# Spare TensorE passes in the last pair of heads and in the routing, and two steps of the pair moved, in a graph-transformer layer

## What is computed

```python
q, k, v = (split(xn @ W.T + b) for W, b in ((Wq, bq), (Wk, bk), (Wv, bv)))     # 16 heads of 64
phi = lambda z: (exp(z @ orf.T / 64 ** 0.25 - |z|^2 / (2 * 8)) + 1e-6) / 16      # 256 features
out = (phi(q) @ (phi(k).T @ v)) / (phi(q) @ sum(phi(k)))
x = x + gnn(xn) + out @ Wo.T + bo
g = softmax(top2(layernorm(x) @ gate_w.T + gate_b))
x = x + sum over e of g[e] * (layernorm(x) @ expert_w[e] + expert_b[e])
```

## Time and profile before

| | us |
|---|---|
| median of 3 runs | 1418.61 (1415.19 to 1418.94) |
| the profiled execution | 1417.75 |
| its span, first to last instruction | 1416.2 |
| mean granted TensorE clock | 0.973 of full |
| TensorE busy | 1354.4 (96%) |
| DVE, ACT, GpSimd busy | 789.3, 572.3, 364.1 |

### The profile page before, as it was taken

One profiled execution on the slowest core, in us unless ns is written; L12 is line 12 of the kernel. 1 busy time (PEld: TensorE's weight loads), 2 busy tenths in 40 slices (PEclk: granted clock), 3 DMA queues, 4 the chain that ended last, 5 costly groups with the idle time before them and its releaser, 6 DMA issues.

```text
span 1416.2 us, 25340 instructions
## 1 busy us (share of the span) xinstructions
PE 1354.4 (96%) x8233; PEld 1197.6 (85%) x8234; DVE 789.3 (56%) x1680; ACT 572.3 (40%) x953; POOL 364.1 (26%) x375
## 2 busy tenths in 40 slices
PE   6999999999999999999999999999999599999996
PEld 3567778999999999999999999987888588888885
DVE  7867464454466565656565656564454734444641
ACT  8543332211355454545454545451122234444440
POOL 4323333254210101010101010005023133333432
PEclk9999999999999999999999999978999599999998
DMA  5112112455200000000000000013244567777853
GB/s 185 51 49 68 42 64 68 134 158 150 64 31 16 30 15 30 15 30 15 30 15 30 15 30 0 1 60 98 72 166 148 208 183 218 220 213 211 287 134 58
DMA packets 58102, 127.78 MB, mean 90 GB/s; under 512 B 7627, under 2 KB 28827, under 8 KB 58049
## 3 DMA queue, kind: packets, MB, share of 16 engines
q1 hardware_dynamic: 48016, 96.79, 20.6%
q0 software_dynamic: 10032, 30.30, 8.7%
HBM read 91.46 MB, written 37.43 MB: 91 GB/s over the span
## 4 chain that ended last, share of the span: by engine, by line
PE 85%; DVE 5%; ACT 3%; issue 3%; DMA 1%; DVEq 0%; POOL 0%; POOLq 0%; SPq 0%; ACTq 0%
PE PB L1701 8%; PE PB L1806 7%; PE PB L1808 7%; PE PB L1807 7%; PE PB L2022 6%; PE PB L2023 6%; PE PB L2025 6%; PE PB L1844 5%; PE PB L1867 4%; PE PB L1751 3%; PE PB L1791 3%; PE PB L1752 3%; PE PB L1753 3%; PE PB L1792 3%; PE PB L1793 2%
## 5 line engine op out<-in xcount | busy, mean ns | idle before, releaser
L1806 PE MATMUL PB<-xh,hw 128*128 128x416 f32 (+1 forms) x576 | 203.8, 354 | 0.0
L1808 PE MATMUL PB<-xh,hw 128*128 128x416 f32 (+1 forms) x576 | 202.9, 352 | 0.0
L1807 PE MATMUL PB<-xl,hw 128*128 128x416 f32 (+1 forms) x576 | 202.8, 352 | 0.0
L2022 PE MATMUL PB<-mwh,mth 128*128 128x512 f32 x368 | 147.8, 402 | 0.3 <-issue 0.3
L2023 PE MATMUL PB<-mwl,mth 128*128 128x512 f32 x368 | 143.9, 391 | 0.0
L719 POOL CAST hw<-hraw 128x1024 fp32r<-128x1024 f32 x24 | 25.2, 1048 | 418.4 <-DVE qphi L1363 197.3
L1701 PE MATMUL PB<-ohs,ohd 128*128 128x512 bf16 x564 | 114.1, 349 | 0.3 <-DVE ohs L1226 0.3
L2025 PE MATMUL PB<-mwh,mtl 128*128 128x512 f32 x368 | 113.7, 390 | 0.0
L1807 PEld LDWEIGHTS PB<-xl,hw 128*128 128x128 f32 x576 | 108.6, 189 | 1.2
L1806 PEld LDWEIGHTS PB<-xh,hw 128*128 128x128 f32 x576 | 108.6, 189 | 1.2
L1808 PEld LDWEIGHTS PB<-xh,hw 128*128 128x128 f32 x576 | 108.5, 188 | 1.0
(11 more groups left out here) (304 smaller groups left out, 3103.7 us busy)
## 6 DMA issues: line engine op xcount, KB each, us to landing
mraw<-expert_w SPq DMA_DIRECT2D x64, 512.0 KB, 5.8
count_rests<-ATf POOLq DMA_DIRECT2D x9, 640.0 KB, 3.3
xrow<-x SPq DMA_DIRECT2D x40, 128.0 KB, 3.0
y_scratch<-xrow SPq DMA_DIRECT2D x40, 128.0 KB, 1.9
yrow<-y_scratch SPq DMA_DIRECT2D x20, 256.0 KB, 2.9
x2n_half<-xhat SPq DMA_DIRECT2D x20, 256.0 KB, 2.4
out<-x SPq DMA_DIRECT2D x9, 512.0 KB
ATf<-wg SPq DMA_DIRECT2D x32, 128.0 KB, 2.8
```

Source lines behind the costliest of these rows:

```text
L1806: mm(bank(i, n), hw[:, wi, 0, k, :], xh[:, k, c0:c0 + n], start=(k == 0), stop=False)
L1807: mm(bank(i, n), hw[:, wi, 0, k, :], xl[:, k, c0:c0 + n], start=False, stop=False)
L1808: ins = mm(bank(i, n), hw[:, wi, 1, k, :], xh[:, k, c0:c0 + n], start=False, stop=(k == KT - 1))
L2022: mm(y[c], mth[:, k, :], mwh[par][:, k, c * CW:(c + 1) * CW], start=(k == 0), stop=False)
```

## The change

- On TensorE, the second head's key chunk 1 stands ahead of the first head's key-value products instead of behind them, in all eight pairs.
- In the first seven pairs, the second head's query chunks 2, 3 and 4 are issued after steps 2, 4 and 6 of the projection third instead of after steps 1, 3 and 5. Chunk 5 stays behind the third.
- In the last pair, 32 spare passes of 512 columns are issued: 9 between the first head's query chunks, 7 between those of the second, 3 + 1 + 2 + 1 ahead of the four groups of transposes and 9 behind them. They write PSUM bank 0, which nothing reads any more.
- In the routing, 36 spare passes on the first expert's weights into bank 6: 4 ahead of the wait for the prefix counts' input, 20 behind these products, 12 ahead of the gates. Before the first four TensorE waits for the first slab of those weights.
- GpSimd waits for the first row tile of the output product between its split of the weights and the routing's constants.

```diff
@@ gpsimd
             split_weights(ro, 1)
+            pool.wait_ge(ro.done, 1)
             g.iota(iota8[:, :, :], [[0, TT], [1, E]], base=0, channel_multiplier=0,
@@ tensor
+            def spare(n):
+
+                for _ in range(n):
+                    mm(bank(0), orfh[:, 0:P], xh[:, 0, 0:CW], start=True, stop=True)
+
             def pair(j, last):
@@
                 turn_values(3)
+                key_features(j, 1, 1)
                 key_values(0, 0, MH * TT)
-                key_features(j, 1, 1)
                 project_third(j, 2, 0)
@@
                 if last:
                     for i in range(2, 6):
+                        spare((0, 0, 0, 2, 5, 2)[i])
                         query_features(0, i)
                     query_features(1, 0)
@@
                 if last:
                     for i in range(2, 5):
+                        spare(2)
                         query_features(1, i)
+                    spare(1)
                 else:
-                    project_third(j + 1, 0, 2, lambda k: query_features(1, 2 + k // 2) if k % 2 == 1 else None)
+                    project_third(j + 1, 0, 2, lambda k: query_features(1, 1 + k // 2) if k in (2, 4, 6) else None)
                 query_features(1, 5)
@@
+                if last:
+                    spare(3)
                 turn(0)
+                if last:
+                    spare(1)
                 turn(1)
                 if not last:
                     key_features(j + 1, 0, 0)
                     project_third(j + 1, 1, 1)
+                if last:
+                    spare(2)
                 turn(2)
+                if last:
+                    spare(1)
                 turn(3)
+                if last:
+                    spare(9)
@@
+            def meanwhile(n):
+
+                for _ in range(n):
+                    mm(bank(6), mwh0[:, 0, 0:P], mwh0[:, 0, 0:CW], start=True, stop=True)
+
+            pe.wait_ge(mw_high, 1)
+            meanwhile(4)
             pe.wait_ge(s_both, 1)
@@
             ins.then_inc(route_done, 1)
-
+            meanwhile(20)
@@
+            meanwhile(12)
             gates(0)
```

## The result

The changed kernel took 1400.05 us in the median of 5 runs (1398.57 to 1407.57), the kernel before 1418.61 us (1412.16 to 1420.43): a ratio of 0.9892, 95% interval 0.9865 to 0.9919. The forecast was 1398.4. By ratio the change is worth 14 to 15 us of the 20.2 that were summed up, by the medians of the first five runs 18.6.

The account below looks back on a forecast made before the run. TensorE, busy 96% of the span, bounds the kernel; time is won only at its waits or half clock. 3.7 + 4.2 + 12.0 + 0.3 = 20.2 us off 1417.75 gives 1397.5, as median 1398.4; range 1394.0 to 1404.5.

Parts of the forecast that it names:

- Key chunk ahead, 3.7 us: Ahead of the key-value products: the chunk fills TensorE's 0.56 us idle time, 0.46 us a pair in eight pairs.
- rival 5: Key-value products: a wait ahead of them lowers the clock in the reshaped pairs, 6.4 us a pair slower; chance 0.02.
- Query chunks one step later, 4.2 us: In the first seven pairs: issuing later covers a 0.49 us wait for ACT, 0.60 us a pair.
- The last pair, 12.0 us: Last pair through the output product's first passes: 32 spare passes keep the clock full, 12.0 us less.
- 4.9 + 0.45 + 4.05 + 0.25: Last pair's gains: to first head's outputs, to second head's outputs, their 40 products, turning the result back.
- busy 1.80 of 3.40 us: Last pair, 932.5 to 935.9: TensorE's busy time, with three waits, before the clock fell.
- narrow products with a wait of 0.49 us among them keep the clock: Ordinary pair: 6.6 us, two thirds of it 65-column products, ran at full clock despite that wait.
- GpSimd's wait, 0 us: GpSimd's wait for the first output row tile is satisfied before it is reached, costing 0.
- The routing, 0.3 us: Routing's 36 spare passes: the clock returns, falls again before the gates; only the first ten gate products gain.
- rival 1: Routing: the clock holds there too, 1.2 us more gained, 1397.2 us; chance 0.12.
- The sentence on idle gaps: Skill page ties a lost clock to longer idle gaps; by it the routing would give 1.5 us, not 0.3.

Follow-up runs that it names:

- query_step_only: Only the query chunks issued one step later, against the kernel before: 1414.51 us, median of 10, ratio 0.9996 [0.9968, 1.0023].
- the later split: Changed kernel with GpSimd's split of the next pair's key weights moved behind the turned values: 1399.02 us, ratio 0.9864 against the kernel before.
- the logits' spares: Changed kernel with the later split and eight spare passes among the last logits: 1400.33 us with 20 passes ahead of the gates, 1398.84 with 12.
- routing_only: Only the routing's 36 spare passes and GpSimd's wait, against the kernel before: 1415.23 us, median of 10, ratio 0.9985 [0.9955, 1.0015].
- chunk_ahead_only: Only the key chunk moved ahead of the key-value products, against the kernel before: 1407.96 us, median of 8, ratio 0.9943 [0.9915, 0.9972].

## Why the prediction was right, and where its terms were not

The median, 1400.05, lies 1.7 us from the forecast and inside its range; the 1404.98 of the six further runs lies 0.5 outside. Its opening says that the longest of TensorE's waits outside the routing is the 2.92 us ahead of the output product. That holds from attention on; before it the list of the kernel before has 6.2 us (line 1675, for DVE) and 4.4 us (line 1720, for ACT), which the change leaves as they are. The steps, in the order of the prediction:

1. *Key chunk ahead, 3.7 us.* The mechanism is shown: no wait, products not delayed, 0.1 us paid by the projection, 0.42 us a pair. The term was mis-sized: alone it gives about 8 us (4 to 12). What it left out is the clock. It had rival 5's price on the wrong side: a wait ahead of the narrow products that brings the clock down is a thing of the order before, seen in two ordinary pairs of `query_step_only`, at 3.2 us each where rival 5 had 6.4, and of the profiles of the new order in the first pair alone. The 10 us less at half clock are worth 3.6 us, which with the pairs' 3.4 nearly makes up the 8. That they are falls at this place is an inference, and the count speaks for a part only: two falls in five profiles are 1.3 us an execution. The execution read had no such fall, so the sum had no such term.
2. *Query chunks one step later, 4.2 us.* 0.5 to 0.6 us a pair is shown. Alone the time does not move, with an interval (4.5 us less to 3.3 more) that takes in the 4.2. Its executions are at half clock for 73 us in the median against 65 of the kernel before, some 2.8 us at 0.35, which would hide most of the gain; whether the move brings more falls or these ten executions had them by chance is open. On top of the key chunk it is worth about 4 us by difference: moves and routing together 14, less 8 for the chunk, less 2 for the routing. That is worked out, not measured by itself.
3. *The last pair, 12.0 us.* The stages came out as computed (48.0 us to the output product against the 57.89 of before less 4.9 + 0.45 + 4.05 + 0.25, which is 48.2), but the term was mis-sized: it took one execution's fall at 935.9 for what every execution does. Measured three ways it is 4.3 us (alone), 2.0 (taken out beside the later split) and 0 to 1 (whole against whole without). Without spares the clock mostly holds to the wait ahead of the output product: of the seven profiles without them one, the one that the prediction read, lost it from 935.9 through to the output product and took 57.9 us to the row tile; the other six took 47.6 to 48.9. All six lost it at that last wait of 3.2 us, for 3 to 7 us, and by these profiles that is what the spares save in most executions. The step that failed is the inference from "busy 1.80 of 3.40 us" to a fall in every execution. The reading of the earlier trace rows that narrow products with a wait of 0.49 us among them keep the clock holds for that execution too; `query_step_only` lost it behind 0.56.
4. *GpSimd's wait, 0 us.* Nothing in the profile of after waits for the constants.
5. *The routing, 0.3 us.* About 2 us by ratio, with an interval that takes in none and the 0.3. The time at half clock falls by some 20 us (68 to 49 in the median; the whole change has 31 in the median of its first runs and 41 in that of the six more), but most of it in a stretch where DVE is the chain, so that it buys little: at 0.35 it would be 6.5 us. The gap ahead of the gates brought the clock down again, against rival 1.

The total was met because the errors lie on opposite sides: 4 us too little at the key chunk, 8 to 12 too much in the last pair, and up to 2 too little in the routing. By the ratios, 14 to 15 us, the sum of 20.2 was 5 too high. That the total landed so near is luck: the largest term was nearly three times too large or more, a gain that the sum did not have stood against it, and kernels whose executions spread by 12 us (after) and 19 us (before) can give a median some microseconds off.

The sentence on idle gaps taken from the Trainium skill ("TensorE: Matmul & The Clock Gate", "Why this matters for your kernels") is answered from both sides here. The clock fell behind a wait of 0.56 us, where that page speaks of longer gaps; and it also held through three waits with one of 1.09 us. The falls around the 3.2 us wait ahead of the output product agree with the page.

Open are where the key chunk's gain in clock lies in the span, the logits' spares, which showed the shortest execution and no better median, and what the last pair's spares save in just those executions in which the clock would fall.

## What to carry to other kernels

Filling a short wait ahead of narrow products with wide work that has to be done anyway can be worth more than the wait: here 0.46 us a pair on paper and about 1 us (0.5 to 1.5) in the runs. The executions then also spent some 10 us less at half clock; a fall in such a wait costs 3.2 us when it comes. Before a stretch at half clock is priced, look at it in several executions, or at least compare the mean granted clock of all runs. And look at what the neighbouring engines run beside the step that is late: one moved loop entry on GpSimd took away the fall in the first pair that three of four profiles of the change, with all, some or none of the last pair's spares, show at its full length.

## What the runs showed of the hardware that was not expected

- The same instructions with the same waits lose the clock in one execution and keep it in another: in the last pair for 34 us from 935.9 on (the kernel before), or only at the wait ahead of the output product (953.5, `routing_only`). With the key chunk moved and the same three waits it was lost for 3.4 us (`chunk_ahead_only`). Before's executions had between 45 and 103 us at half clock.
- Products of 65 columns, back to back, neither bring a full clock down by themselves nor a low one up: 40 of them took 4.6 to 4.7 us at full clock throughout where no wait stood ahead, 8.63 at half clock throughout, and 6.28 with the fall among them behind a wait of 0.56 us, and the clock rose only under the wide passes behind.
- A DVE addition of 128x512 elements took 2.00 to 2.03 us in place of 0.43 beside a GpSimd subtraction of 2.37 us, in all nine profiles in which both ran at once in the first pair, and 0.43 once they were apart.
